# Scores on VectorE, no unread TensorE products after the first step, and a new order on every engine

## The chip, the cores and the metric

The kernel runs on one core of a Trainium2 chip. The metric is the time of the whole program on the device, in microseconds (us), as the median of several runs. Lower is better.

## What is computed

The reference is two adaptive-norm layers over 16 batch elements of 256 tokens and 128 channels, all in float32. Each layer has an attention part and a feed-forward part, and both are added back with a gate:

```python
h = _layernorm(x) * (1 + ca) + sa
x = x + ga * _L0_attn_ref(h, ...)      # 16 heads of 8 channels, softmax over 256 keys
h = _layernorm(x) * (1 + cb) + sb
x = x + gb * _L0_ffn_ref(h, ...)       # 16 experts, top 4 of them weighted by a softmax
...
h = _layernorm(x) * (1 + ca) + sa
x = x + ga * _L1_attn_ref(h, ...)      # running sums over time of value * phase rotor
h = _layernorm(x) * (1 + cb) + sb
x = x + gb * _L1_ffn_ref(h, ...)       # token shift, sigmoid and squared relu
```

The change touches the expert part of the first layer. All 16 experts are computed for every token, and the top-4 scores (zero for the other experts) scale each expert's hidden activation:

```python
gate = jnp.minimum(gu[..., ::2], LIMIT)
up = jnp.clip(gu[..., 1::2], -LIMIT, LIMIT)
glu = gate * jax.nn.sigmoid(gate * ALPHA)
act = (up + 1.0) * glu
expert_out = jnp.einsum('tei,eih->teh', act, down_proj) + down_bias
out = jnp.einsum('te,teh->th', scores, expert_out)
```

## The kernel before

Everything lies in on-chip memory as 128 channels by 256 tokens, one batch element at a time. The program is a software pipeline of three batch elements. A step(a, b, nx) runs the attention and the experts of element a (layer 0), the whole second layer of element b = a - 1, and the start of element nx = a + 1: its load, first norm, the q and k products, and the first scores. There is a head and a `first` for element 0, then `step(1, 0, 2)`, a hardware loop `Fori(2, 15)` with 13 passes, `step(15, 14, None)`, and `last(15)`.

Nothing schedules the work at run time. Each engine runs the calls of its own `step` in the order in which they are written, and an instruction waits at the head of its engine's queue until the semaphores that `need(...)` names have come. So the order of the calls is the schedule. The pieces that matter here:

- **Attention of a.** `scores(n)` and `maxima(n)`, n = 0 to 7: TensorE makes four heads of scores at a time in one half of the PSUM tile `ring`, VectorE (DVE in the profile) reduces them to row maxima `smax`. `split_max`, `turn_max`, `copy_max` and the DMA `spread_max` put the maxima into two rows of `q_rows`. Then `scores_t(n)`, `exps(n)` (ScalarE, ACT in the profile) and `values(n)`. `copy_values` writes `o_raw`, which is a part of `sc_all`. `turn_values`, `attn_norm`, `attn_out_1/2`, `attn_tail/attn_tail_2` and GpSimd's `residual1` end it in `x1`.
- **Rows of nx.** For the scores q and k have to stand three times over in bf16 parts on other partitions. ACT's `part` and `part_2` and GpSimd's `rest_q` and `rest_q_2` make the parts `qk_part`, and `spread(nx)` on the SyncE queue (SPq) issues 18 DMAs of 64 KB into `q_rows` and `k_rows`. `scores(nx, 0)` waits for all 18.
- **Router and experts of a.** Second norm, `router`, `route`/`route_2` on VectorE make the scores `sc` and their three bf16 parts; `turn_scores` and `copy_scores` turn them; `broadcast(n)` spreads the scores of four experts over the partitions and `copy_broadcast(n)` copies them to `sc_all`. For each pair n of experts: TensorE's `gate_up(n)` into `ring`, ACT's `gate_clip`, `bend` (silu, into `gsc`), `up` and `clip_up` (into `upc`, a part of `prob`), GpSimd's `expert_pair(n)` multiplies `gsc` by `sc_all`, VectorE's `expert_last(n)` multiplies by `upc`, and TensorE's `down_pair(n)` sums into `pa`. `experts_out` ends it in `x2`, and the third norm (`mean`, `centre3`, `square`, `variance`, `epsilon`, `deviation`, `scale`, `modulate`) gives the second layer its input `hb`.
- **Second layer of b.** Four column groups c = 0 to 3: `phases`/`phase`/`memory_a`/`tables` make the sines and cosines, `phase_values`/`value` and `time_values` the values, `memory_p/_b/_c/_d/_o/_s/_s12` on VectorE and `sums_1/2` on TensorE the running sums, `memory_wo(c)` adds the projection into `pb`. `memory_end`, the fourth norm and `mix_...` end it.
- **Unread products.** `warm(n, bank)` runs n float32 products of 256 columns whose result nobody reads. A step has five of them: two in `warm_scores` and three (`WARM`) in `broadcast(a, 0, nx)`. `warm_last` adds ten in the step without nx.

A float32 product of 256 columns shows as two passes on TensorE (PE). GpSimd (POOL) cannot read PSUM, and reads `gsc` and `sc_all` from SBUF, as VectorE can. The two calls that swap engines and the fillers in question are these:

```python
def expert_pair(b, n):                     # POOL, line 421
    need(pool, "silu", b, n + 1)
    if n % 2 == 0:
        need(pool, "bc", b, n // 2 + 1)
...
def warm_scores(b, n):                     # PE, line 722
    need(pe, "ya", b, 1)
    warm(n, ring[:, 1, :])
```

## Time and profile before

| what | value |
|---|---|
| runs | 1394.96, 1395.64 and 1398.1 us |
| median | 1395.64 us |
| span of the profiled execution | 1390.0 us |
| the profiled execution's own time | not listed apart from the three runs; the median is 5.6 us over the span |
| PE busy | 1248.1 us, 90% of the span |
| VectorE busy | 1136.3 us, 82% |
| ACT busy | 970.5 us, 70% |
| POOL busy | 280.8 us, 20% |
| mean granted TensorE clock | 0.994 of full speed |
| one pass of the loop | 81.2 us |

How to read it. The span runs from the first to the last instruction; what the median has beyond it is launch and end. PE's share is high, but its busy time holds the unread products as well. A busy share alone does not tell what ends a step: the engines wait for each other in a fixed order, so the places where PE stands still, and what ends each of these waits, tell more than the shares.

### The profile page before, as it was taken

What the parts mean: (1) busy time and instruction counts of PE and PEld (TensorE: products, weight loads), DVE (VectorE), ACT (ScalarE), POOL (GpSimd) and SP (SyncE); (2) the same over time, 40 slices, a digit from 0 to 9 for tenths busy, and PEclk for the clock granted to TensorE, in tenths of its full rate; (3) what the DMA queues carried; (4) which work ended last, traced back from release to release, by engine and by line L of the source; (5) the groups of instructions that cost most, each with busy time, mean ns of one, the idle gap of its engine ahead of it and who ended that gap; (6) DMA issues with size and microseconds to landing.
All of it is one profiled execution on the core that took longest, in us unless ns stands there. A gap on an engine that the chain in (4) does not pass through costs nothing.

```text
span 1390.0 us, 22686 instructions
## 1 busy us (share of the span) xinstructions
PE 1248.1 (90%) x7130; PEld 938.9 (68%) x7130; DVE 1136.3 (82%) x2104; ACT 970.5 (70%) x1699; POOL 280.8 (20%) x258
## 2 busy tenths in 40 slices
PE   7798998989899898989989898998989899898989
PEld 5475775758577575757758575775857577585778
DVE  7758879797987979798797979879797987979765
ACT  1665767778676777867677786767778676776841
POOL 4030221303022130302213031221303122130200
PEclk9899999999999999999999999999999999999999
DMA  5330301204030110403012030301204030120000
GB/s 126 93 35 5 35 9 16 20 8 34 8 34 8 15 19 8 34 8 32 10 13 21 8 34 8 31 10 13 21 8 34 8 31 11 12 22 5 1 4 4
DMA packets 54392, 29.82 MB, mean 21 GB/s; under 512 B 3725, under 2 KB 53338, under 8 KB 54362
## 3 DMA queue, kind: packets, MB, share of 16 engines
q1 hardware_dynamic: 52472, 28.74, 17.2%
q10 hardware_dynamic: 1890, 0.70, 0.5%
q8 instruction: 16, 0.26, 0.1%
q14 instruction: 14, 0.11, 0.0%
HBM read 8.20 MB, written 2.10 MB: 7 GB/s over the span
## 4 chain that ended last, share of the span: by engine, by line
PE 56%; DVE 14%; ACT 14%; issue 10%; POOL 2%; DMA 1%; SPq 1%; ACTq 1%; DVEq 0%; POOLq 0%
PE ring L762 15%; PE pb L862 7%; PE pa L776 7%; DVE smax L1814 5%; PE pa L680 4%; PE ring L667 3%; PE ring L716 3%; PE pb_k L792 2%; DVE prod L1927 2%; ACT prob L1279 2%; PE ring L749 2%; PE ring L629 2%; PE pb_v L820 1%; ACT L1383 1%; ACT frac L1386 1%
## 5 line engine op out<-in xcount | busy, mean ns | idle before, releaser
L427 POOL TENSOR_TENSOR gsc<-gsc,sc_all 128x512 f32<-128x512 f32 x128 | 175.7, 1377 | 353.2 <-ACT gsc L1344 353.2
L762 PE MATMUL ring<-ht,wgu 128*128 128x256 f32 x1024 | 241.5, 384 | 1.0 <-ACT sc_all L1332 1.0
L1954 DVE TENSOR_TENSOR_SCAN prod<-keep,prod 128x512 f32<-128x512 f32 x188 | 224.2, 1214 | 0.0
L762 PEld LDWEIGHTS ring<-ht,wgu 128*128 128x128 f32 x1024 | 193.2, 191 | 34.8 <-issue 5.0
L1814 DVE TENSOR_REDUCE smax<-ring 128x4 f32<-128x1024 f32 x128 | 153.3, 1219 | 17.6 <-PE ring L629 10.8
L1887 DVE SCALAR_TENSOR_TENSOR prob<-prob,gsc 128x512 f32<-128x512 f32 x120 | 81.4, 688 | 81.9 <-POOL gsc L427 63.5
L862 PE MATMUL pb<-prod,wo 128*128 128x256 f32 x544 | 129.3, 382 | 5.9 <-DVE prod L1968 5.8
L1279 ACT ACTIVATE prob<-ring 128x1024 f32<-128x1024 f32 x128 | 125.7, 1024 | 5.1 <-PE ring L667 3.5
L1339 ACT ACTIVATE gsc<-ring,gub_t 128x256 f32<-128x256 f32 x256 | 110.5, 501 | 21.3 <-PE ring L762 21.0
L776 PE MATMUL pa<-prob,wdown 128*128 128x256 f32 x512 | 122.0, 380 | 1.8 <-DVE prob L1881 1.8
L862 PEld LDWEIGHTS pb<-prod,wo 128*128 128x128 f32 x544 | 102.0, 190 | 25.2 <-DVE prod L1968 12.0
L1350 ACT ACTIVATE prob<-ring,gub_t 128x256 f32<-128x256 f32 x240 | 103.5, 499 | 8.9 <-PE pa L776 7.0
L776 PEld LDWEIGHTS pa<-prob,wdown 128*128 128x128 f32 x512 | 95.9, 190 | 15.3 <-DVE prob L1881 3.0
L1344 ACT ACTIVATE gsc<-gsc,gate_top 128x512 f32<-128x512 f32 x128 | 95.1, 760 | 0.3
L1355 ACT ACTIVATE prob<-prob,up_top 128x512 f32<-128x512 f32 x120 | 87.5, 770 | 0.0
L680 PE MATMUL pa<-prob,vt 128*32 128x256 f32 x1024 | 76.9, 394 | 10.3 <-ACT prob L1279 8.4
L667 PE MATMUL ring<-q_rows,k_rows 128*128 128x256 bf16 x512 | 73.7, 277 | 11.8 <-ACT prob L1279 10.4
L1332 ACT ACTIVATE sc_all<-ring 128x1024 f32<-128x1024 f32 x64 | 63.5, 1023 | 23.4 <-DVE prod L1949 16.2
L792 PE MATMUL pb_k<-hb,wk 128*128 128x256 f32 x256 | 68.6, 390 | 12.2 <-ACT hb L1242 11.5
L667 PEld LDWEIGHTS ring<-q_rows,k_rows 128*128 128x128 bf16 x512 | 42.8, 98 | 49.9 <-ACT prob L1279 29.6
L629 PE MATMUL ring<-k_rows,q_rows 126*128 126x256 bf16 x480 | 70.2, 276 | 6.3 <-ACT prob L1350 3.0
L420 POOL TENSOR_TENSOR x<-xt,ya 128x256 f32<-128x256 f32 x16 | 11.6, 727 | 305.0 <-ACT ya L1306 305.0
(284 smaller groups left out, 2476.1 us busy)
## 6 DMA issues: line engine op xcount, KB each, us to landing
q_rows<-qk_part SPq DMA_DIRECT2D x144, 64.0 KB
k_rows<-qk_part SPq DMA_DIRECT2D x135, 64.0 KB
x_in<-in_L_attn_x_dram SPq DMA_DIRECT2D x16, 128.0 KB, 2.1
sc_all<-_L_ffn_gate_up_proj_dram SPq DMA_DIRECT2D x1, 2048.0 KB, 11.9
out_dram<-xo SPq DMA_DIRECT2D x16, 128.0 KB, 1.8
prob<-in_L_wmod_dram SPq DMA_DIRECT2D x2, 384.0 KB, 3.9
k_rows<-qk_part ACTq DMA_DIRECT2D x9, 64.0 KB
wo<-in_L_attn_Wo_dram SPq DMA_DIRECT2D x1, 512.0 KB, 7.4
```

What stands on the lines that cost most here:

```text
L427: pool.tensor_tensor(gsc[:, n % NG, :], gsc[:, n % NG, :], sca, ALU.mult).then_inc(S["gsc"], 1)
L629: last = mm(ring[:, n % 2, j * L:(j + 1) * L], lhsT=q_rows[0:P - 2, h, (n // 4) * P:(n // 4 + 1) * P], rhs=k_rows[0:P - 2, h, :], start=Tr ...
L667: last = mm(ring[:, (n + 1) % 2, j * L:(j + 1) * L], lhsT=k_rows[:, h, (n % 2) * P:(n % 2 + 1) * P], rhs=q_rows[:, h, :], start=True, stop ...
L680: last = mm(pa[32 * j:32 * (j + 1), o:o + L], lhsT=vt[:, n % 2, 4 * (n // 2) + j, :], rhs=prob[:, n % NPT, j, :], start=(n % 2 == 0), stop ...
L762: last = mm(ring[:, n % 2, g * 512 + j * L:g * 512 + (j + 1) * L], lhsT=wgu[:, 2 * n + j, g, :], rhs=ht[:, :], start=True, stop=True, skip ...
L776: last = mm(pa[:, 0:L], lhsT=wdown[:, 2 * n + j, :], rhs=upc[:, n % NU, j * L:(j + 1) * L], start=False, stop=(n == 7 and j == 1), skip_gr ...
L862: last = mm(pb[:, 0:L], lhsT=wo[:, n // 2, 2 * c + j, :], rhs=prod[:, c % 2, n, j * L:(j + 1) * L], start=(c == 0 and n == 0 and j == 0), ...
L1279: af(prob[:, n % NPT, :, :].rearrange("p i q -> p (i q)"), ring[:, (n + 1) % 2, :], ACT.Exp).then_inc(S["prob"], 1)
L1339: af(gsc[:, n % NG, j * L:(j + 1) * L], ring[:, n % 2, j * L:(j + 1) * L], ACT.Relu, scale=-1.0, bias=gub_t[:, 0, 2 * n + j:2 * n + j + 1] ...
L1350: af(upc[:, n % NU, j * L:(j + 1) * L], ring[:, n % 2, 512 + j * L:512 + (j + 1) * L], ACT.Relu, scale=-1.0, bias=gub_t[:, 1, 2 * n + j:2 ...
L1814: nc.vector.tensor_reduce(smax[:, n // 4, 4 * (n % 4):4 * (n % 4) + 4], ring[:, n % 2, :].rearrange("p (h k) -> p h k", h=4), AX_X, ALU.ma ...
L1954: nc.vector.tensor_tensor_scan(prod[:, h, n - 1, :], keep[:, :], prod[:, h, n - 1, :], 0.0, ALU.mult, ALU.add).then_inc(S["cu" + str(n)], 1)
```

## The change

Four things are changed.

1. In every step the product of silu and spread score, `gsc * sc_all`, is made by VectorE (`expert_mul`) in place of GpSimd (`expert_pair`). `first` keeps GpSimd's.
2. `warm_scores` and `broadcast` run their unread products only for element 0, so each of the 15 steps has five fewer. `warm_last` is gone (ten in the last step). In `last` four are moved to its start, four between the mean and the variance are dropped, and four stand behind the last transposes in place of ahead of them.
3. The calls of every engine are put in another order.
4. The boundary of the loop pass lies elsewhere: `scores(nx, 7)`, `turn_max(nx)` and the first `phases`, `phase_values` and `time_values` of the second layer end a step, where they began the next one. VectorE's `scale(.., "3", ..)`, `next_b` and `maxima(.., 4)` begin a step, where they ended one.

The waits that were calls of their own (`rows_landed`, `values_free`, `weights_loaded`, `tables_ready`, `weights_copied`) stand inside the calls that need them, for element 0.

```diff
@@ gpsimd, step
                 if on_x:
                     rest_q(nx)
                     rest_q_2(nx)
-                if on_a:
-                    expert_pair(a, 0)
...
-                    expert_pair(a, 6)
                 if on_b:
                     deviation(b, "4", vepsb, rstdb)
                 if on_a:
-                    expert_pair(a, 7)
                     deviation(a, "3", vepsb, rstdb)
@@ vector
+            def expert_mul(b, n):
+                need(dve, "silu", b, n + 1)
+                need(dve, "bc", b, n // 2 + 1)
+                sca = sc_all[:, 2 * n:2 * n + 2, :].rearrange("p e t -> p (e t)")
+                tt(gsc[:, n % NG, :], gsc[:, n % NG, :], sca, ALU.mult).then_inc(S["gsc"], 1)
@@ tensor
             def warm_scores(b, n):
                 need(pe, "ya", b, 1)
-                warm(n, ring[:, 1, :])
+                if is_first(b):
+                    warm(n, ring[:, 1, :])
...
-                    warm(WARM, ring[:, 0, :])
+                    if is_first(b):
+                        warm(WARM, ring[:, 0, :])
@@ tensor, first
-                turn_max(a)
                 turn_inv()
                 turn_bias()
+                turn_max(a)
@@ sync, step
-                if nx is not None:
+                if on_a:
+                    spread_max(a)
+                if on_x:
                     load_x(nx)
-                if a is not None:
-                    spread_max(a)
-                if nx is not None:
                     spread(nx)
```

The rest of the diff is the order of the calls. Three places of it are shown as the instructions of the loop pass.

The first is ACT's queue from the router to the experts, before the change. `qk_part<-qk` is `part` and `part_2`, `sin_t`, `frac`, `cos_t` are `tables(b, 3)`, `sctb` and `sct` are `copy_scores`, and `sc_all<-ring` is `copy_broadcast`.

```order
L1259 ACTIVATE qk_part<-qk 128x512
L1242 ACTIVATE ht<-cent,mod_a 128x256
L1264 ACTIVATE qk_part<-qk 128x512
L1375 ACTIVATE sc_all<-pb_k 128x512
L277 REGISTER_ALU
L1317 ACT_TABLE_LOAD
L1317 ACTIVATE ex<-lsh 128x32
```

And the same place of ACT's queue after it, from `route` on:

```order
L1298 ACTIVATE ex<-lsh 128x32
L1299 ACT_TABLE_LOAD
L1299 ACTIVATE silu<-gate_top 128x1
L1364 ACTIVATE sin_t<-frac 128x2x256
L1367 ACTIVATE frac<-frac 128x512
L1371 ACTIVATE cos_t<-frac,half_pi 128x2x256
L287 REGISTER_ALU
L1241 ACTIVATE qk_part<-qk 128x512
L287 REGISTER_ALU
L1304 ACTIVATE sctb<-ring 48x256
L1306 ACTIVATE sct<-ring 16x256
```

`part` stood ahead of `route`'s exponential and stands behind it and behind `tables(b, 3)` now. `part_2` moves further, to between the third and the fourth copy of the spread scores:

```order
L1313 ACTIVATE sc_all<-ring 128x1024
L1246 ACTIVATE qk_part<-qk 128x512
L287 REGISTER_ALU
L1313 ACTIVATE sc_all<-ring 128x1024
L287 REGISTER_ALU
L1320 ACTIVATE gsc<-ring,gub_t 128x256 x2
```

So the rows of nx can only be issued once three of the four score copies are through, just ahead of the first `gate_clip`.

The second place is PE's queue between the router and the first `gate_up`. Before (`ring<-upper,ident` are the unread products, `pb<-prod,wo` is `memory_wo`, `ring<-sctb,sel` is `broadcast`):

```order
L716 MATMUL ring<-upper,ident 128x256 x2
L862 MATMUL pb<-prod,wo 128x256 x4
L731 MATMUL ring<-ident,sc 16x128 x2
L733 MATMUL ring<-identb,sc_part 48x128 x2
L716 MATMUL ring<-upper,ident 128x256 x3
L749 MATMUL ring<-sctb,sel 128x256 x8
L827 MATMUL pb_k<-upper,prod 128x256
```

And after it:

```order
L859 MATMUL pb<-prod,wo 128x256 x4
L824 MATMUL pb_k<-upper,prod 128x256
L826 MATMUL pb_k<-upper,prod 128x128
L824 MATMUL pb_k<-upper,prod 128x256
L826 MATMUL pb_k<-upper,prod 128x128
L727 MATMUL ring<-ident,sc 16x128 x2
L729 MATMUL ring<-identb,sc_part 48x128 x2
L746 MATMUL ring<-sctb,sel 128x256 x4
```

The running sums `sums_1(b, 2)` (`pb_k<-upper,prod`) moved ahead of the turned scores, and no product stands where the five unread ones were.

The third place is VectorE's queue in the expert stage, after the change (`gsc<-gsc,sc_all` is `expert_mul`, `prob<-prob,gsc` is `expert_last`, `prod<-keep,prod` is a scan of `memory_c`):

```order
L1870 TENSOR_TENSOR gsc<-gsc,sc_all 128x512
L1942 SCALAR_TENSOR_TENSOR prod<-keep,prod 128x512 x2
L1875 SCALAR_TENSOR_TENSOR prob<-prob,gsc 128x512
L287 REGISTER_ALU
L1870 TENSOR_TENSOR gsc<-gsc,sc_all 128x512
L1927 TENSOR_TENSOR prod<-prod,cos_r 128x512
L1875 SCALAR_TENSOR_TENSOR prob<-prob,gsc 128x512
L1942 SCALAR_TENSOR_TENSOR prod<-keep,prod 128x512
```

Each `expert_last` now has its own `expert_mul` ahead of it on the same queue, most with one or two pieces of the second layer between them.

## Rows read from the trace of the kernel before

**Rows 1.** Page, the span and part 1, busy us of each engine.

```profile
span 1390.0 us, 22686 instructions
...
PE 1248.1 (90%) x7130; PEld 938.9 (68%) x7130; DVE 1136.3 (82%) x2104; ACT 970.5 (70%) x1699; POOL 280.8 (20%) x258
```

**Rows 2.** Windows: sum, PE, PEld, DVE, ACT, POOL, clock, DMA share, GB/s; one pass.

```profile
600.40:681.60 81.20, 73.74 (x430) 55.15 (x429) 68.62 (x126) 60.34 (x107) 16.80 (x15) 1.00 0.17 18
```

**Rows 3.** Timeline, start and us, around the two groups of unread products.

```profile
639.56 1.03 PE L716 MATMUL ring<-upper,ident 128*128 128x256 f32 x4
...
641.01 1.99 PE L862 MATMUL pb<-prod,wo 128*128 128x256 f32 x8 [0.41 <-DVE prod L1968]
...
643.60 1.56 PE L716 MATMUL ring<-upper,ident 128*128 128x256 f32 x6
...
644.43 0.36 ACT L1323 ACTIVATE sctb<-ring 48x256 bf16<-48x256 bf16 x1
...
645.10 1.04 PE L749 MATMUL ring<-sctb,sel 48*128 48x256 bf16 x8
```

**Rows 4.** Groups by line and shape: busy, mean ns, idle before.

```profile
L1887 DVE SCALAR_TENSOR_TENSOR prob<-prob,gsc 128x512 f32<-128x512 f32 x120 | 81.4, 688 | 81.9 <-POOL gsc L427 63.5 <-ACT prob L1355 18.2
...
L1974 DVE TENSOR_TENSOR prod<-prod 128x512 f32<-128x512 f32 x60 | 41.0, 684 | 0.0
```

**Rows 5.** Timeline, a POOL product beside a VectorE product, both from SBUF.

```profile
659.10 1.64 POOL L427 TENSOR_TENSOR gsc<-gsc,sc_all 128x512 f32<-128x512 f32 x1 [0.88 <-ACT gsc L1344]
659.53 1.77 DVE L1962 TENSOR_TENSOR prod<-prod,cos_t 128x512 f32<-128x512 f32 x1
```

**Rows 6.** Timeline, nine places of one pass.

```profile
609.50 0.71 SPq L308 DMA_DIRECT2D q_rows<-m_sb  x1
...
612.00 1.04 PE L667 MATMUL ring<-q_rows,k_rows 128*128 128x256 bf16 x8
...
614.59 4.98 ACT L1279 ACTIVATE prob<-ring 128x1024 f32<-128x1024 f32 x5
...
624.67 0.60 ACT L1295 ACTIVATE sc_all<-pa 128x512 f32<-128x512 f32 x1 [0.76 <-PE pa L680]
...
630.49 0.72 POOL L420 TENSOR_TENSOR x<-xt,ya 128x256 f32<-128x256 f32 x1 [19.69 <-ACT ya L1306]
...
638.36 0.19 DVE L1836 TENSOR_TENSOR lg<-ring,rbias 128x32 f32<-128x32 f32 x1 [0.21 <-PE ring L707]
...
649.30 3.72 PE L762 MATMUL ring<-ht,wgu 128*128 128x256 f32 x16
...
672.98 1.03 PE L629 MATMUL ring<-k_rows,q_rows 126*128 126x256 bf16 x8 [0.21 <-ACT prob L1350]
...
678.66 0.41 DVE L1759 TENSOR_TENSOR centb<-x,pb 128x256 f32<-128x256 f32 x1
```

**Rows 7.** Timeline, the last part of q and k and the first DMA of rows.

```profile
638.25 1.16 POOL L414 TENSOR_TENSOR qk_part<-qk,qk_part 128x512 bf16<-128x512 f32 x1 [1.29 <-ACT qk_part L1264]
...
639.43 0.63 SPq L303 DMA_DIRECT2D q_rows<-qk_part  x1
```

**Rows 8.** Windows, end of the row DMAs issued from 476.93 and 720.69 on.

```profile
496.93:497.93 1.00, 1.00 (x7) 0.87 (x6) 1.00 (x2) 1.00 (x4) 1.00 (x1) 1.00 0.18 13
...
744.69:745.69 1.00, 1.00 (x6) 0.90 (x5) 0.00 (x0) 1.00 (x4) 1.00 (x1) 1.00 0.08 4
```

**Rows 9.** First step: timeline, then a window behind that wait, clock 0.61.

```profile
38.53 0.29 PE L546 MATMUL pb<-ident,gsc 16*128 16x16 f32 x2 [1.02 <-DVE gsc L1696]
...
107.30 1.78 PE L629 MATMUL ring<-k_rows,q_rows 126*128 126x256 bf16 x8 [1.26 <-DMA k_rows<-qk_part]
...
107.30:108.00 0.70, 0.70 (x4) 0.52 (x5) 0.00 (x0) 0.00 (x0) 0.00 (x0) 0.61 0.00 0
```

**Rows 10.** Timeline, the last step: a rstd and the products that wait behind fillers.

```profile
1328.31 0.69 POOL L402 TENSOR_TENSOR rstdb<-vepsb,mhalf 128x2 f32<-128x2 f32 x1 [5.25 <-DVE vepsb L1763]
...
1329.71 0.61 PE L584 MATMUL pb<-ident,rstdb 128*128 128x128 f32 x4
```

More of the change, by code:

```diff
@@ L959, in step @@
                 if on_b:
-                    memory_wo(b, 0)
+                    phases(b, 3)
                 if on_x:
-                    head_3(nx)
+                    head_1(nx)
                 if on_a:
@@ L1133, in first @@
                 scores(nx, 5)
+                phases(a, 0)
+                phase_values(a, 0)
                 scores(nx, 6)
-            def last(b):
-                phases(b, 0)
-                phase_values(b, 0)
-                phases(b, 1)
-                time_values(b, 0)
-                phase_values(b, 1)
+                scores(nx, 7)
+                time_values(a, 0)
+                phases(a, 1)
+                turn_max(nx)
+                phase_values(a, 1)
+            def last(b):
+                warm(4, ring[:, 0, :])
                 time_values(b, 1)
@@ L1477, in step @@
                     tables(b, 3)
+                if on_x:
+                    part(nx)
                 if on_a:
@@ L1557, in first @@
                 copy_broadcast(a, 2)
+                part_2(nx)
                 copy_broadcast(a, 3)
-                part(nx)
-                part_2(nx)
                 gate_clip(a, 0)
@@ L2026, in step @@
                 on_a, on_b, on_x = a is not None, b is not None, nx is not None
+                if on_b:
+                    scale(b, "3", centb, pb)
+                    next_b(b)
                 if on_a:
+                    maxima(a, 4)
                     maxima(a, 5)
-                    maxima(a, 6)
+                    next_a(a)
                 if on_b:
@@ L2156, in step @@
                     maxima(nx, 3)
-                    maxima(nx, 4)
                 if on_b:
                     mix_out(b)
-                if on_a:
-                    scale(a, "3", centb, pb)
-                    next_b(a)
             def first(a, nx):
@@ L2215, in first @@
                 maxima(nx, 3)
-                maxima(nx, 4)
-                scale(a, "3", centb, pb)
-                next_b(a)
             def last(b):
+                scale(b, "3", centb, pb)
+                next_b(b)
                 memory_a(b, 0)
```

419 lines of the change are left out of this document (204 added, 215 removed).

## The prediction, on record before the run

> **What bounds the kernel now.** I read the busy times first. PE is busy for 1248 of 1390 us, VectorE for 1136, POOL for 281 [rows 1]. One pass of the hardware loop takes 81.2 us and holds 73.7 us of PE, 68.6 of VectorE, 60.3 of ACT and 16.8 of POOL, at full TensorE clock [rows 2]; so PE stands still for 7.5 us of a pass and VectorE for 12.6. No engine is full, and the end of a pass is set by a chain that changes engine. I therefore read the idle time by line, then the timeline of one pass. I measure places in it from the third norm's first instruction (`centre3`, 678.66 here, so 597.41 one period of 81.25 earlier) [rows 6]. On that scale the softmax exponentials start at 17.2, the second `copy_values` is at 27.3, POOL's residual `x` at 33.1, the router's logits at 40.9, the first `gate_up` at 51.9, the first scores of nx at 75.6, the next `centre3` at 81.25.
>
> **The expert products.** One of VectorE's waits stands out: 63.5 us of the 81.9 ahead of `expert_last` end with POOL's product, which is 63.5 / 15 = 4.2 us a step [rows 4]. VectorE now gets eight products of its own. A product of 128x512 f32 from SBUF took it 0.684 us [rows 4], so 8 x 0.684 = 5.5 us are added. POOL loses its eight. Where both read SBUF at once, a VectorE product took 1.77 us in place of 0.68 and POOL's 1.64 [rows 5]; this one collision a pass gives back 1.1. VectorE goes from 68.6 to about 73.0 us a pass. What hides it is the 12.6 us that VectorE idles [rows 2], 4.2 of them just these waits for POOL. That cover is thin in the expert stage; were it gone, the net cost would be 5.5 - 1.1 - 4.2 = 0.2 us a pass. I take zero, since PE has 22 us of products queued there.
>
> The Trainium skill (SBUF — State Buffer, two separate sides) calls the shared port pair an exclusive lock: the loser waits for the whole instruction. By it up to eight of POOL's products could each block VectorE for one, and the relief would be up to eight times 1.1, 8.8 us. The trace shows one stretched VectorE product in a pass, so it does not bear that out.
>
> **The unread products.** Five f32 products are ten PE passes, 1.03 + 1.56 = 2.6 us a step [rows 3]. But PE's next product behind the first group waits 0.41 us for VectorE even with them, and the turned scores behind the second group are ready at 644.43 + 0.36 = 644.79, against the product's 645.10 [rows 3]. So at most 0.3 us of the second group is on the path. PE goes to 73.7 - 2.6 = 71.1 us a pass. The gain is bounded by zero and 2.6; I take 0.3, and it is inside the walk below.
>
> **The new order, up to the experts.** I walked each engine's new queue with the durations of the old timeline.
> - Exponentials: 17.2 to 16.0. VectorE's `scale` and `next_b` stand ahead of the fifth maxima, so `hb` comes 1.2 us earlier and ACT's sines no longer end last. What is late next is the DMA of maxima rows, 2.5 us from its issue to PE's use [rows 6].
> - From there to the second `copy_values`: 10.05 to 9.9. ACT's phases leave the gap between exponentials, but PE's running sums stand behind the second turned scores and cost 0.35.
> - To POOL's `x`: 5.85 to 5.1, because the sine table load no longer stands ahead of the attention output.
> - To the logits: 7.85 to 7.3. VectorE's copy of x is out of the norm; a `memory_wo` on PE ahead of the norm's last product costs about 0.8 of that again.
> - To the first `gate_up`: 10.95 to 11.2. Here ACT has `tables(b, 3)` (2.0 us) and `part` (0.6) ahead of `copy_scores`, which eats what the unread products gave.
>
> Together the first `gate_up` starts 2.4 us earlier, at 49.5. Behind it PE had 23.7 us until the scores of nx (672.98 - 649.30 [rows 6]) and has 22.05 now, with the bias products moved ahead and one variance moved out. So PE could start these scores at 71.55, in place of 75.6.
>
> **The rows of nx: the new wait.** Before, the last part of q and k ended at 639.41, on my scale 42.0, and the first of 18 row DMAs was issued at once [rows 7]. Issue to landing took between 20.75 and 24.2 us in 13 passes, 22.6 in the mean; the shortest and the longest end in [rows 8]. They landed some 11 us before PE used them, so nothing waited. Now `part` stands behind the router's exponential and `tables(b, 3)`, and `part_2` behind three of four score copies. By my walk the last part ends at 51.15, 1.65 us after the first `gate_up`. The rows land at 51.15 + 22.6 = 73.75, and `scores(nx, 0)`, ready at 71.55, waits 2.2 us. Queued behind it on PE are the down products and the norm of `x2`. On this branch the time from the scores to the next `centre3` is 5.65 + 1.3 = 6.95 us: VectorE's mixing now stands between `experts_out` and `centre3`, and one more group of scores ahead of the mean. The period comes to 73.75 + 6.95 = 80.7 us, against 81.25. That is 0.55 a pass, and for 14 steps with rows 7.7 us. Slips of PE, VectorE or ACT in the expert stage up to 2.2 us cost nothing there, since the rows are awaited anyway.
>
> **Outside the steady passes.** Step 15 has no nx and so no rows: it keeps the whole 2.35 us, and 1.2 for `warm_last` (the reciprocal root is ready at 1329.0, the product behind the fillers runs at 1329.71 [rows 10], and a second group costs as much), 3.5 in all. In `last`, unread products ahead of the variance and of the last transposes go: 1.0. In the first step the rows are issued some 2.7 us earlier, and the wait of 1.26 us at 107.30 goes [rows 9]; `turn_bias` ahead of `turn_max`, near PE's wait at 38.53 [rows 9], delays the maxima, of which 1.2 stays: 1.5 net. Sum 6.0; bounds 2 and 9.
>
> **The clock.** All steady passes ran at full clock, with no PE gap over 1.0 us. In the first step, behind gaps of 0.70, 1.12 and 1.26 us, the granted clock fell: 0.61 of full in the window behind the last one [rows 9], and stayed at 1.2 GHz until 110.8, at a cost of at most 1.7 us. The new row wait of 2.2 us is longer than those gaps, and the unread products that kept PE busy are gone. Bounds: zero, and 1.7 x 14 = 24 us. I take 0.3 a pass, nearer zero because the work on either side of the wait is dense (73.7 of 81.2), which the first step's is not: 4.2 us.
>
> **Sum.** The profiled execution's own time is not listed apart; its span is 1390.0, and the median of the runs, 1395.64, is 5.6 above it. Changes of the span are carried to the median as they stand: 1395.64 - 7.7 - 6.0 + 4.2 = 1386.1, said as 1386.0. The mean row time alone moves it by (24.2 - 22.6) x 14 = 22 us up or (22.6 - 20.75) x 14 = 26 down (down to where PE binds), though single passes average out.
>
> **Rivals.**
> A. *The rows do not bind.* They land as PE wants them, because `part_2` runs earlier than my walk puts it or 18 DMAs go faster beside a quieter POOL. Then the period is 81.25 - 2.35 = 78.9, and the time 1395.64 - 14 x 2.35 - 6 = 1356.7. For it: 11 us of slack before. Against it: the queue's order says plainly that the parts come some 9 us later. Chance 0.13.
>
> B. *The row wait halves the clock: slower.* Place: `scores(nx, 0)`. Each pass then runs what follows at 1.2 GHz, as the first step did from 107.4 to 110.8. At the full 1.7 us a pass, with the late rows eating the 7.7 (they land at 24.2 rather than 22.6, or the parts slip by 0.55 more), the time is 1395.64 + 24 - 6 - 7.7 to + 24 - 6, so 1406 to 1414. It decides as soon as the loss exceeds 1.0 us a pass. For it: [rows 9]. Against it: that was a stage with three gaps near each other. The Trainium skill (TensorE: Matmul & The Clock Gate, section HAM oscillation) tells of a kernel whose TensorE waits for a DMA in every tile and restarts at the low clock each time; by it this is what each pass would do. The first step's rows agree with it, and no row of a steady pass shows a wait that long. Chance 0.22.
>
> C. *VectorE becomes the bound, so the change does not do what it says.* With 73.0 of 80.7 us busy and each `expert_last` behind its product and one or two scans, its queue would set the pace of the down products. Net 0.2 us a pass beyond before, and nothing of the order's gain: 1395.64 + 3 = 1399, less or more by what the ends give. For it: the 63.5 us wait is replaced by work on the same engine. Against it: VectorE has only 0.68 where POOL had 1.64 [rows 5] and a hand-over. Chance 0.10.
>
> My forecast, rows bind and part of the gain stays, has 0.55.
>
> **Numbers.** The range is 1362 to 1408: it leaves out most of A's low end and B's high end. About 0.2%, 2.8 us, is what a measurement of this kernel can tell from no change, so faster means below 1392.8 and slower above 1398.4. Faster gets A's 0.13 and 0.41 of the forecast's 0.55, together 0.54. Same gets 0.10 of the forecast and 0.06 of B and C. Slower gets the rest of B and C, 0.26, and 0.04 of the forecast: 0.30.
>
> **What would show it.** Right: a period near 80.7; a wait of about 2 us for a DMA at PE's first scores of nx, in every pass but the last; the first `gate_up` 49.5 after `centre3`, the last part 1.6 behind it; the third norm starting 7 us behind these scores; PE near 71, VectorE near 73 and POOL near 6 us a pass; no wait of `expert_last` for POOL; the product that took 1.77 back at 0.68; granted clock near 1.00. Wrong: no DMA wait there (A), a clock clearly under 1.00 in steady passes (B), PE waiting for `prob` from VectorE through the expert stage (C), or `gate_up` not earlier than 51.

## The result, and the profile after

The changed kernel takes 1419.8 us (median of four runs, 1410.5 to 1439.2), the kernel before 1395.6. The ratio, 1.0146 with a 95% interval of 1.0125 to 1.0168, is of the fast runs alone and leaves out the one of 1439.2. So the change is slower by 20 us by the ratio and by 24 by the medians. The forecast was 1386, range 1362 to 1408, with 0.30 for slower.

The page, span and busy times:

```profile
span 1420.3 us, 22302 instructions
...
PE 1268.9 (89%) x6960; PEld 951.5 (67%) x6960; DVE 1212.2 (85%) x2224; ACT 971.2 (68%) x1699; POOL 137.9 (10%) x138
```

Against [rows 1], VectorE grew by 76 us and POOL halved, both in the direction foreseen. VectorE takes 73.9 us a pass, not 73.0: the 1.1 us of relief did not come. The product that took 1.77 us is back at 0.68, but in the pass from 613.14 two others now run beside GpSimd's `rest_q` and `rest_q_2` and take 1.65 and 1.13 us in place of 0.68. And PE is 21 us busier with 170 products fewer. The windows of two passes, measured from `centre3` to `centre3` (columns as in [rows 2]: clock, DMA share and GB/s at the end), say why:

```profile
526.63:613.14 86.51, 76.24 (x419) 57.04 (x419) 73.89 (x135) 60.38 (x107) 7.20 (x7) 0.92 0.18 17
...
866.94:947.87 80.93, 74.01 (x419) 55.09 (x419) 73.81 (x135) 60.39 (x107) 7.21 (x7) 0.96 0.16 18
```

The granted clock is 0.92 to 0.96 in every steady pass, where it was 1.00 [rows 2], and passes of one program now take anything from 80.9 to 86.7 us. The 14 passes with rows take 1163.6 us together, 83.1 each, against 81.2. That is 27 of the 30 us between the spans; the first step adds 1.3 us and step 15 another 2.0. The spans lie further apart than the medians because the profiled execution of the kernel before was a short one. In every run listed with its span the time is only 1.7 or 1.8 us above the span, so of the 5.6 us between span and median of the kernel before some 4 are that difference and not launch and end. Its granted clock of 0.994 is above the 0.988 to 0.993 of the same kernel's later runs too. PE's longest waits, in all, how often, and the longest:

```profile
PE ring L620 <- DMA k_rows<-qk_part: 18.6, 12, 5.1
PE ring L661 <- DMA q_rows<-m_sb: 18.0, 15, 1.3
PE ring L746 <- ACT sc_all L1313: 15.5, 20, 1.2
PE ring L746 <- ACT sctb L1304: 15.1, 15, 1.1
```

There are three places a pass: the first scores of nx (L620), the first turned scores, waiting for the maxima rows (L661), and the spread scores (L746), where the unread products stood. The timeline at the three, the last two in the pass from 866.94, the first in that from 526.63:

```profile
880.59 1.05 PE L661 MATMUL ring<-q_rows,k_rows 128*128 128x256 bf16 x8 [1.15 <-DMA q_rows<-m_sb]
...
911.24 0.59 PE L746 MATMUL ring<-sctb,sel 48*128 48x256 bf16 x4 [1.07 <-ACT sctb L1304]
...
603.92 1.46 PE L620 MATMUL ring<-k_rows,q_rows 126*128 126x256 bf16 x6 [3.33 <-DMA k_rows<-qk_part]
```

And the windows behind the last two of these:

```profile
913.94:919.94 6.00, 6.00 (x17) 3.78 (x18) 5.93 (x10) 3.27 (x4) 1.16 (x1) 0.50 0.06 14
...
603.86:610.00 6.14, 6.08 (x23) 5.11 (x24) 2.67 (x5) 0.29 (x1) 0.69 (x1) 0.50 0.00 0
```

Both run at 0.50, which is 1.2 GHz. Such a stretch is called a drop below. One stands at the spread scores in every pass and takes in the first `gate_up`; one at the first turned scores comes in nine of 15 passes; one at the row wait in the four that waited over 1.5 us. Neither of the first two places has a single wait: PE stands still for 0.57, 0.66 and 1.15 us within 4 us at the turned scores of the pass from 866.94, and for 1.07 and 0.88 us within 4 us at its spread scores.

The last reading is of the rows. SPq issued the first at 577.46. Windows around their end:

```profile
601.00:602.00 1.00, 0.00 (x0) 0.00 (x0) 0.90 (x2) 0.93 (x3) 0.00 (x0) 1.00 0.41 24
602.00:603.00 1.00, 0.00 (x0) 0.00 (x0) 0.00 (x0) 0.00 (x0) 0.00 (x0) 1.00 0.00 0
603.00:604.00 1.00, 0.08 (x1) 0.09 (x2) 0.00 (x0) 0.00 (x0) 0.00 (x0) 0.64 0.00 0
```

The queues fall silent before 602.0, some 24 us behind the issue, which is the long end of [rows 8]. PE starts at 603.92, about 2 us behind the last packet, and for most of that time no engine works. The trace also keeps the times of the semaphore updates that the transfers send, though no view lists them. Over the 14 passes with rows the last one comes 22.2 to 26.4 us behind the issue, 24.2 in the mean, which is 1.0 to 2.1 us behind the last packet. Where PE waits it starts 0.05 us behind that update. From issue to PE it is 26.5 us here, and 24.6 to 26.5 in the four passes that waited over 1.5 us.

VectorE's groups, as in [rows 4]:

```profile
L1870 DVE TENSOR_TENSOR gsc<-gsc,sc_all 128x512 f32<-128x512 f32 x120 | 82.4, 688 | 49.6 <-ACT gsc L1325 49.4
...
L1875 DVE SCALAR_TENSOR_TENSOR prob<-prob,gsc 128x512 f32<-128x512 f32 x120 | 82.2, 685 | 3.2
```

The 63.5 us of waiting for POOL are gone. VectorE now waits for ACT and is not the bound.

### The profile page after: what moved, and what is told of

It reads as the page before. It is cut to its first block, busy times and chain, and to the rows that moved or that the text cites. A ratio compares the mean times of both kernels' runs of the same rounds, so it can differ in the third digit from the quotient of the medians.

```text
span 1420.3 us, 22302 instructions
## 1 busy us (share of the span) xinstructions
PE 1268.9 (89%) x6960; PEld 951.5 (67%) x6960; DVE 1212.2 (85%) x2224; ACT 971.2 (68%) x1699; POOL 137.9 (10%) x138
## 4 chain that ended last, share of the span: by engine, by line
PE 40%; DVE 16%; DMA 14%; ACT 10%; SPq 9%; issue 8%; POOL 3%; ACTq 0%; DVEq 0%; POOLq 0%
DMA k_rows<-qk_part 11%; SPq L313 9%; PE ring L661 4%; PE ring L759 4%; PE pb L859 4%; PE pa L773 4%; DVE prod L1937 4%; PE pa L676 3%; DVE smax L1796 3%; PE pb_k L789 3%; DMA q_rows<-m_sb 2%; PE pb_v L824 2%; ACT prob L1261 1%; DVE prod L1910 1%; PE ring L620 1%
## 5 line engine op out<-in xcount | busy, mean ns | idle before, releaser
L759 PE MATMUL ring<-ht,wgu 128*128 128x256 f32 x1024 | 266.1, 414 | 1.1
L759 PEld LDWEIGHTS ring<-ht,wgu 128*128 128x128 f32 x1024 | 212.1, 210 | 48.5 <-issue 14.2
L773 PE MATMUL pa<-prob,wdown 128*128 128x256 f32 x512 | 133.4, 396 | 0.0
L1870 DVE TENSOR_TENSOR gsc<-gsc,sc_all 128x512 f32<-128x512 f32 x120 | 82.4, 688 | 49.6 <-ACT gsc L1325 49.4
L1331 ACT ACTIVATE prob<-ring,gub_t 128x256 f32<-128x256 f32 x240 | 110.1, 556 | 0.1
L859 PEld LDWEIGHTS pb<-prod,wo 128*128 128x128 f32 x544 | 101.0, 190 | 12.5
L1325 ACT ACTIVATE gsc<-gsc,gate_top 128x512 f32<-128x512 f32 x128 | 105.3, 824 | 0.2
L661 PE MATMUL ring<-q_rows,k_rows 128*128 128x256 bf16 x512 | 81.6, 298 | 21.4 <-DMA q_rows<-m_sb 18.0
L1336 ACT ACTIVATE prob<-prob,up_top 128x512 f32<-128x512 f32 x120 | 95.3, 816 | 0.0
L661 PEld LDWEIGHTS ring<-q_rows,k_rows 128*128 128x128 bf16 x512 | 47.0, 105 | 63.3 <-issue 42.0
L620 PE MATMUL ring<-k_rows,q_rows 126*128 126x256 bf16 x480 | 67.6, 280 | 18.7 <-DMA k_rows<-qk_part 18.6
L1224 ACT ACTIVATE hb<-centb,mod_b 128x256 f32<-128x256 f32 x32 | 19.2, 601 | 94.4 <-DVE centb L1749 57.9
L412 POOL TENSOR_TENSOR rstdb<-vepsb,mhalf 128x2 f32<-128x2 f32 x32 | 22.5, 703 | 562.5 <-DVE vepsb L1745 562.5
```

The lines of the kernel that those rows point to most:

```text
L661: last = mm(ring[:, (n + 1) % 2, j * L:(j + 1) * L], lhsT=k_rows[:, h, (n % 2) * P:(n % 2 + 1) * P], rhs=q_rows[:, h, :], start=True, stop ...
L759: last = mm(ring[:, n % 2, g * 512 + j * L:g * 512 + (j + 1) * L], lhsT=wgu[:, 2 * n + j, g, :], rhs=ht[:, :], start=True, stop=True, skip ...
L773: last = mm(pa[:, 0:L], lhsT=wdown[:, 2 * n + j, :], rhs=upc[:, n % NU, j * L:(j + 1) * L], start=False, stop=(n == 7 and j == 1), skip_gr ...
L859: last = mm(pb[:, 0:L], lhsT=wo[:, n // 2, 2 * c + j, :], rhs=prod[:, c % 2, n, j * L:(j + 1) * L], start=(c == 0 and n == 0 and j == 0), ...
L1325: af(gsc[:, n % NG, :], gsc[:, n % NG, :], ACT.Silu, scale=-ALPHA, bias=gate_top[:, 0:1]).then_inc(S["silu"], 1)
L1331: af(upc[:, n % NU, j * L:(j + 1) * L], ring[:, n % 2, 512 + j * L:512 + (j + 1) * L], ACT.Relu, scale=-1.0, bias=gub_t[:, 1, 2 * n + j:2 ...
```

## The experiments

All kernels are stated against the kernel before, run on the same chip beside them (1395.9 to 1397.2 us).

**First four: the unread products and the late rows, one by one.** `after_fillers_back` puts the five products of a step back.

```diff
 def warm_scores(b, n):
     need(pe, "ya", b, 1)
-    if is_first(b):
-        warm(n, ring[:, 1, :])
+    warm(n, ring[:, 1, :])
@@ broadcast, n == 0
-                    if is_first(b):
-                        warm(WARM, ring[:, 0, :])
+                    warm(WARM, ring[:, 0, :])
@@ tensor, step
                     sums_2(b, 2)
+                if on_a:
+                    warm_scores(a, 2)
+                if on_b:
                     memory_wo(b, 1)
```

> The changed kernel with the five unread products of every step put back where they stood (two ahead of the turned scores, three ahead of the first spread of scores). Theory A (the clock: the wait of 1.07 us ahead of the spread scores, where the unread products stood, drops TensorE to 1.2 GHz for 6.8 us in every pass, and this is the larger cost): the drop behind the turned scores is gone in every pass, PE's busy time falls by 2 to 3 us a pass although work is added, and the time is 1385 to 1400 us. Rival B (the row wait is the main cost, the clock hardly matters): the clock comes back, but the time stays at 1410 us or more, since the rows are issued at the same place. Rival C (VectorE is the bound): no change, 1415 to 1425.

Its four runs took 1412.6, 1441.8, 1448.0 and 1459.1 us. Rival B's bound, 1410 us or more, held: in the profile, which is of the shortest run, the clock is back at 0.94 to 0.98 a pass, and the time is no better. PE is earlier at the scores of nx and the rows are not, so it waits longer there (22.8 us in all, against 18.6), and four passes have a drop at that wait, which is on the path. Whether this kernel is slower than the changed one is open, since its shortest run lies among the changed kernel's.

`after_parts_early` issues the rows earlier, at 48.2, where passes of the changed kernel with a drop at the turned scores issue them at 52.5 and those without at 50.8.

```diff
                 if on_a:
                     route(a)
-                if on_b:
-                    tables(b, 3)
                 if on_x:
                     part(nx)
+                if on_b:
+                    tables(b, 3)
                 if on_a:
                     copy_scores(a)
-                    copy_broadcast(a, 0)
-                    copy_broadcast(a, 1)
-                    copy_broadcast(a, 2)
                 if on_x:
                     part_2(nx)
                 if on_a:
+                    copy_broadcast(a, 0)
+                    copy_broadcast(a, 1)
+                    copy_broadcast(a, 2)
                     copy_broadcast(a, 3)
```

> The changed kernel with part directly behind the router's exponential, ahead of the last tables, and part_2 directly behind copy_scores, ahead of all four copies of the spread scores; no unread products. The rows are issued some 5 us earlier. Theory A (clock at the score turn is the larger cost): the DMA waits of 18.6 us at the first scores of nx go to under 2, with the clock drops behind them, but the drop behind the turned scores stays in every pass: 1398 to 1410 us. Rival B (rows are the main cost): 1385 to 1395 us. Rival C (VectorE): 1415 or more.

1403.9 us (1400.9 to 1406.2), ratio 1.0045 [1.0028, 1.0062], as theory A had it. The row waits of the passes are gone (4.7 us stay in the first step) and so is the spread of the runs. But nearly every pass took 81.9 us at a clock of 0.94, with a drop at the turned scores and one at the spread scores in every one.

> Both edits. Theory A: no row wait, and no clock drop but one behind the wait for the maxima rows: the period comes near 79.5 us and the time to 1370 to 1380 us. Rival B: the same as with the early parts alone, within 3 us. Rival C (VectorE is the bound at 73.5 us busy): not under 1395.

This has both edits. 1408.3 us, ratio 1.0081 [1.0064, 1.0097]: neither theory A's 1370 to 1380 nor within rival B's 3 us. Rival C's bound, not under 1395, is met, and the next pair of runs tells against it. One pass, and the clock behind the wait for the maxima rows and around the last spread of scores:

```profile
602.66:684.55 81.89, 76.25 (x429) 57.13 (x429) 74.20 (x134) 60.54 (x107) 7.19 (x7) 0.96 0.17 18
615.50:619.00 3.50, 2.69 (x11) 2.05 (x12) 3.50 (x6) 3.47 (x5) 0.00 (x0) 0.57 0.15 39
651.50:655.30 3.80, 3.23 (x13) 1.96 (x13) 3.77 (x8) 2.85 (x3) 0.00 (x0) 0.77 0.47 64
```

Two drops were left, behind a wait of 1.14 us for the maxima rows and behind one of 0.57 us ahead of the last spread. That made the next pair of edits.

`before_no_fillers` is the kernel before with `if` b is element 0 ahead of both `warm` calls, as the change has it.

> The kernel before with nothing changed but the five unread products of a step left out (those of the first step stay, and the ten of the last step). Theory A (the unread products hold the clock): a wait of 1 us or more appears on PE ahead of the spread scores, the clock falls behind it in most passes, and the time is 10 to 35 us over the kernel before, 1405 to 1430. Rival (they only matter in the new order, whose queue of ACT is later there): clock stays full, 1391 to 1397 us, as the 0.3 us a step of the prediction says.

1404.6 us (1400.6 to 1411.1), ratio 1.0061 [1.0031, 1.009], just under the low edge of theory A. Its timeline and two of its passes:

```profile
480.51 1.96 PE L864 MATMUL pb<-prod,wo 128*128 128x256 f32 x8 [1.38 <-DVE prod L1970]
...
484.35 1.03 PE L751 MATMUL ring<-sctb,sel 48*128 48x256 bf16 x8 [1.27 <-ACT sctb L1325]
```

```profile
436.79:522.74 85.95, 76.30 (x420) 56.70 (x419) 68.78 (x126) 60.61 (x107) 16.13 (x15) 0.94 0.18 17
...
605.44:686.54 81.10, 71.46 (x420) 53.55 (x419) 69.62 (x126) 60.39 (x107) 16.29 (x15) 1.00 0.18 18
```

The waits of 1.38 and 1.27 us stand in every pass of the loop, where the unread products had covered all but 0.41 us of them. In seven of the 13 loop passes the clock holds and the pass is 81.1 us, 0.15 shorter than before, which is what the prediction's 0.3 was about. In five it falls, and they take 82.7 us, in one more 86.0. The products are worth having for the clock alone.

**Second four: fill the two places, then move the expert products.** `maxima_filled` adds two products.

```diff
                 if n == 0:
...
-                    need(pe, "m_rows", b, 16)
                     need(pe, "s_max", b, ST)
+                    warm(2, ring[:, 1, :])
+                    need(pe, "m_rows", b, 16)
```

> after_fillers_and_parts with two more unread products on PE in every step, behind the last maxima and ahead of the wait for the maxima rows (1.2 us in which PE stands still, behind which the clock fell in every pass there). Theory A (the clock drops, not the waits, hold this order back): the drop 12 to 13 us after centre3 is gone, the exponentials start about 1.7 us earlier after it, and with the second drop staying the period is 80.2 us, the time 1380 to 1388 us. Rival B (the pass is bound by VectorE, 74 us busy, or by its waits; the clock is only a symptom): the period stays 81.9 us and the time within 3 us of 1408.

1371.6 us (1367.7 to 1379.5), ratio 0.9838 [0.9793, 0.9884]: 37 us for two products that nobody reads, more than theory A gave. The wait of 1.14 us is 0.25 now, no pass has the drop behind it, and seven of the 13 loop passes have no drop at all, though the wait of 0.57 us ahead of the last spread is still in each. Theory A had the second drop stay everywhere. The timeline at that wait, a pass without a drop and one with the second:

```profile
599.75 1.03 PE L712 MATMUL ring<-upper,ident 128*128 128x256 f32 x4
601.02 1.05 PE L662 MATMUL ring<-q_rows,k_rows 128*128 128x256 bf16 x8 [0.25 <-DMA q_rows<-m_sb]
```

```profile
587.40:666.10 78.70, 73.95 (x433) 55.84 (x433) 73.96 (x135) 60.46 (x107) 7.19 (x7) 1.00 0.17 19
666.10:746.01 79.91, 75.25 (x433) 57.16 (x433) 74.10 (x134) 60.77 (x107) 7.19 (x7) 0.98 0.17 18
```

`maxima_and_spread_filled` moves a real product into the other wait.

```diff
                     broadcast(a, 2)
-                    broadcast(a, 3)
                     down_bias(a)
+                    broadcast(a, 3)
```

> maxima_filled with down_bias moved ahead of the last spread of scores, where PE waited 0.57 us for ACT's copy. Theory A: both drops are gone in every pass, granted clock 1.00, period 78.5 to 79.5 us, time 1357 to 1372 us. Theory A2 (the products of 48 rows there leave TensorE too little work, whatever the wait): the second drop stays, as in maxima_filled within 3 us. Rival B: the period stays 81.9 us.

1358.5 us (1356.3 to 1361.3), ratio 0.9732 [0.9704, 0.976]. Theory A, in all its numbers for the loop (step 15 keeps a drop of 6.8 us):

```profile
582.68:661.19 78.51, 73.93 (x433) 55.85 (x433) 73.97 (x135) 60.55 (x107) 7.19 (x7) 1.00 0.18 19
```

All 13 passes of the loop run at full clock and take 78.4 to 78.5 us, with VectorE busy for 74.0 of them. So VectorE was not the bound at 81.9, which rules out rival B here and rival C of the first four. The second drop did not stay, where theory A2 had expected it to. The moved product fills the wait and puts other work between the products of 48 rows at once, so this pair of runs does not part the two.

`filled_pool_products` gives the eight products of a step back to GpSimd, where the kernel before has them.

```diff
@@ gpsimd, step
                     rest_q_2(nx)
+                if on_a:
+                    expert_pair(a, 0)
...
+                    expert_pair(a, 7)
@@ vector, step
-                if on_a:
-                    expert_mul(a, 0)
...
-                    expert_mul(a, 7)
```

> maxima_and_spread_filled with the eight products of silu and spread score back on GpSimd in the steps (expert_pair), nothing else. If the move to VectorE is what helps (it removed 4.2 us a step of waits for POOL): 10 to 30 us slower than maxima_and_spread_filled. If VectorE at 74 us busy had become the bound: faster by 5 us or more. If the expert stage is bound by PE either way: within 3 us.

1413.4 us, ratio 1.0122 [1.0092, 1.0151]: 55 us slower, beyond the first case's 30. Its group on VectorE:

```profile
L1886 DVE SCALAR_TENSOR_TENSOR prob<-prob,gsc 128x512 f32<-128x512 f32 x120 | 122.4, 1030 | 58.6 <-POOL gsc L437 58.6
```

VectorE waits 58.6 us for POOL again, and its own product takes 1030 ns in the mean instead of 688 [rows 4]. The two engines now meet in the expert stage more often than once a pass: in the pass from 607.93 five VectorE products of 0.68 us take 1.70 to 1.77. That is what the Trainium skill (SBUF — State Buffer, two separate sides) says of the shared port pair, and the row agrees in kind: 342 ns more for each of 120. Passes at full clock take 81.8 us, 3.3 more than 78.5; that is 46 of the 55 us. Four of the 13 loop passes have a drop besides, so not all of the 55 is the expert stage.

`before_products_dve` makes only that part of the change: each product directly ahead of its `expert_last`, in the old order. The other seven pairs are moved as the one shown.

```diff
@@ vector, step
+                    expert_mul(a, 0)
                     expert_last(a, 0)
...
@@ gpsimd, step
-                    expert_pair(a, 0)
...
```

> The kernel before with only the eight products of silu and spread score moved to VectorE, each directly ahead of its expert_last; old order, all unread products. The prediction's 0.2 us a pass at most (5.5 added, 4.2 and 1.1 had back): 1391 to 1399 us. Rival (each product stands on VectorE's path because the second layer's pieces behind it come later): 1405 us or more.

1424.1 us, ratio 1.0184 [1.0149, 1.022]: 27 us slower, the rival. A pass and the group that waits:

```profile
615.15:698.08 82.93, 74.51 (x430) 55.12 (x429) 72.53 (x134) 60.52 (x107) 5.81 (x7) 1.00 0.18 18
```

```profile
L1884 DVE SCALAR_TENSOR_TENSOR prob<-prob,gsc 128x512 f32<-128x512 f32 x120 | 83.1, 692 | 45.4 <-ACT prob L1346 35.9 <-DVE gsc L1879 3.1
```

The clock is full in every pass of the loop. A pass is 1.7 us longer, and all of it lies behind the first `gate_up`, which starts at 51.9 as before: the scores of nx start at 76.6 instead of 75.6, and the next `centre3` another 0.7 later. Over 14 passes that is 24 us. `expert_last` still waits 45.4 us, now for ACT. So the products on VectorE cost 27 us in the old order, and giving them back costs 55 in the new one, which was written for them.

**Last six: the prices, taken from the good side.** `filled_no_five` takes the five products out again, `filled_parts_late` puts `part` and `part_2` back where the change has them; both edits were shown above the other way round.

> maxima_and_spread_filled without the five unread products at the score turn; the two at the maxima wait, the early parts and down_bias ahead of the last spread stay. What the five are worth in this order. The prediction's price (0.3 us a step had back by leaving them out): 2 to 6 us faster than maxima_and_spread_filled. The clock theory: the wait of 1.1 us ahead of the spread scores comes back, the clock falls behind it for 3.4 to 6.8 us in every pass, and the time is 1380 to 1400 us, at least 20 us slower.

1389.6 us (1387.5 to 1390.0), ratio 0.9947 [0.993, 0.9963], 31 us slower. The wait ahead of the spread scores is back, and with it the clock:

```profile
803.75 0.59 PE L747 MATMUL ring<-sctb,sel 48*128 48x256 bf16 x4 [1.07 <-ACT sctb L1305]
```

```profile
759.45:840.69 81.24, 74.55 (x423) 55.93 (x423) 74.26 (x135) 60.38 (x107) 7.62 (x7) 0.96 0.17 18
```

> maxima_and_spread_filled with part and part_2 back where the change has them (behind the last tables, and between the third and fourth copy of the spread scores). What the late rows cost where no other place drops the clock. The prediction's step (the rows are issued 51 us after centre3, land 22.6 us later and bind): a DMA wait of 2 us or more at the first scores of nx in most passes, a period of 80.5 us or more, and the clock falling behind the longer waits: 1385 to 1405 us. Rival (the rows do not bind, rival A of the prediction): within 5 us of maxima_and_spread_filled.

1431.9 us (1412.2 to 1451.0), ratio 1.0169 [1.0104, 1.0235]; all four runs are above the 1405 expected. PE waits for the rows in all 14 passes that have them, and in the first step; the profile is of its longest run:

```profile
PE ring L620 <- DMA k_rows<-qk_part: 59.7, 15, 6.3
```

To part the wait from the clock behind it, two kernels add unread products to `filled_parts_late`, ahead of the wait for the rows:

```diff
-                if n == 0:
-                    need(pe, "qk_rows", b, 16 * 18)
...
+                if n == 0:
+                    warm(6, ring[:, 0, :])
+                    need(pe, "qk_rows", b, 16 * 18)
```

> filled_parts_late with six more unread products on PE ahead of the wait for the rows (2.6 us, about the shortest of the waits there). It parts the wait from the clock that falls behind it. If the wait itself is the price of the late rows (issue at 51.05, PE let go 24.6 to 26.5 us later, against 71.9 where PE could start, and 6.6 us from there to the next centre3, 82.3 to 84.2 us a pass): 1410 to 1432 us, the clock in the passes at 0.98 or more, and only 0 to 20 us had back. If the clock behind the wait is the larger part of it: 1395 us or less.

> The same with ten products (4.3 us). PE is then free at 76.2 us, near the middle of the landings: clock 1.00 in nearly every pass, a remaining wait under 1 us on average. If the wait is the price: within 8 us of the run with six, 1405 to 1430 us. If the clock is: further down with the second drop gone, 1395 us or less.

1404.7 us with six (ratio 1.0064 [1.0046, 1.0082]), 1421.3 with ten (1.0189 [1.0169, 1.021]). The late rows cost 73 us by the medians and 61 by the ratios; six products bring 27 or 15 of that back, which lies between my two cases. The products themselves can only hold PE up, and only one drop at the row wait is left, so part of the price was the clock. How large a part is not shown: between the two profiles the rows also got faster, from 25.3 us to 24.3 in the mean from issue to last semaphore update, some 13 us over 14 passes. What remains is the 2.6 us of products in each pass (36 us), 6.7 us of waits, and a drop at the spread scores in eight passes. Ten are longer than most of the waits and cost 17 us again: inside the first case's range, though not within 8 us of the run with six.

`after_maxima_filled_only` is the changed kernel with the two products of maxima_filled and nothing else.

> The changed kernel with nothing but two unread products ahead of the wait for the maxima rows. The drop 12 to 13 us after centre3, which came in about half of the passes, is gone; the one at the score turn and the row wait stay. Theory (each drop costs about half its length, but where the rows bind, time had back earlier only lengthens the row wait, since gate_up and part_2 hang on the same score copies): 1405 to 1420, no clear difference from the changed kernel. Rival (it is the maxima wait that started the trouble): under 1400.

1399.5 us (1384.2 to 1408.6), ratio 1.001 [0.998, 1.0041]. The theory's 1405 was too high and the rival's bound is just met: two unread products alone bring the changed kernel back to the time of the kernel before, 19 us by the ratios and 20 by the medians. The drop at the score turn in every pass and row waits of 0.6 to 3.1 us in eight are still in its profile, which is of its longest run.

The last tries for more, at both ends of the program.

```diff
@@ act, first
                 route(a)
+                part(nx)
                 down_scaled()
                 copy_scores(a)
-                part(nx)
+                part_2(nx)
                 copy_broadcast(a, 0)
                 copy_broadcast(a, 1)
                 copy_broadcast(a, 2)
-                part_2(nx)
@@ tensor, step
+                if on_a and not on_x:
+                    need(pe, "norm2", a, 1)
+                    warm(2, pa[:, L:2 * L])
                 if on_a:
                     broadcast(a, 1)
```

> maxima_and_spread_filled, with part and part_2 of the first step moved ahead in the same way as in the steps, and two unread products in the last step where head_6 has no work. The row wait of 8.5 us in the first step falls to about 5, and the clock drop in the middle of the last step is gone: 3 to 7 us faster than maxima_and_spread_filled, 1352 to 1356 us. If the rows of the first step land no earlier, or the drop only moves: within 2 us.

1356.8 us (1352.8 to 1358.1), ratio 0.9712 [0.9691, 0.9733]. The first step ends 5.9 us earlier. But two passes had a row wait of 1.1 us that the profile of maxima_and_spread_filled does not have, and two others a drop, so most of it did not stay. The drop in the middle of the last step is gone, and a shorter one stands at its end. By its number this is the second case, within 2 us, and the intervals of the two overlap. Both are 2.7 to 2.9% faster than the kernel before, and some 4% faster than the change.

The drop in the loop is worth a look, since both waits are filled there. PE's longest wait ahead of it, and the windows before it and in it:

```profile
1100.02 0.67 PE L767 MATMUL pa<-sct,dbias 16*128 16x256 f32 x2 [0.37 <-DVE vt L1796]
```

```profile
1097.60:1101.10 3.50, 3.13 (x21) 1.75 (x19) 3.50 (x5) 2.96 (x3) 0.81 (x1) 1.00 0.18 38
1101.10:1104.50 3.40, 3.40 (x10) 2.72 (x9) 3.33 (x6) 1.02 (x1) 0.00 (x0) 0.50 0.66 47
```

What PE ran before it fell were mostly the spread's products of 48 rows and `down_bias` with 16. The same calls with the same wait kept the clock in the other 12 passes of the loop. So a wait of 1 us is not needed for a drop, and theory A2 has a part in this place that no run here parts from the waits.

## Why the prediction was wrong

**The walk was right to within 1.3 us a stage, and in part by luck.** Where the first drop is absent the exponentials start at 15.2, the second `copy_values` at 25.2, the residual at 30.3, the logits at 37.5 and the first `gate_up` at 50.0, and at 49.4 once the waits are filled; foreseen were 16.0, 25.9, 31.0, 38.3 and 49.5. The last part of q and k ends at 50.8 against 51.15. In maxima_and_spread_filled the scores of nx start at 71.9, against 71.55 for PE without a wait, and the next `centre3` comes 6.6 us behind them, against 6.95. The stages that were off made up for each other: the exponentials came 0.8 us early, and from the logits to the first `gate_up` it took 12.5 us (11.8 in the filled kernel) for 11.2. Without waits and drops the order is worth in each pass what rival A gave it, a period of 78.5 where it said 78.9. That its 1356.7 us for the whole comes so near the 1358.5 is luck: between the two profiles the passes gave 5.5 us more than it said, and the ends, for which it took off 6.0, cost 2.9. In the changed kernel itself this gain was never had.

**The rows: a term mis-sized.** "The rows land at 51.15 + 22.6 = 73.75." The 22.6 us reached to the last packet. PE is let go by the last semaphore update, 24.2 us behind the issue in the mean. In the kernel before nothing waited for the rows in a steady pass, so no view of those passes showed the 1.7 us between the two; its trace has them (24.3 us in the mean to the last update, against 22.6). With 24.2 the same sum gives 51.15 + 24.2 + 6.95 = 82.3 us a pass, which is 1.05 x 14 = 15 us slower than before, not 7.7 faster. The sign of the likeliest case hung on this term. Of the 83.1 us that a pass took, 51.7 go to the issue, 24.4 from there to PE's start and 7.0 from there to `centre3`. So 1.8 of the 2.4 us by which 80.7 fell short is this term, and 0.6 is the issue, which a drop at the turned scores puts off by 1.7 us in eight of the passes.

**The clock: wrong place and wrong size.** I allowed 0.3 us a pass, behind the row wait alone. The clock fell at waits of 1.07 and 1.15 us too, each with one or two shorter ones within 4 us ahead of it or behind it, in a pass where PE is otherwise busy. The kernel before had one of 1.00 us without a drop, and its nearest wait over 0.5 us is 12 us away. The prediction had put the first step's drop down to "three gaps near each other"; the new order makes such a place at the turned scores of every pass, and I did not look for one. That the nearness decides is not shown: no run moved a neighbour alone. "At most 0.3 us of the second group is on the path" was true of the path and false as a price: the five products are worth 31 us in the filled kernel and 8 in the old order. I had seen that the new order issues nothing where they stood, and that ACT's `tables` and `part` come ahead of `copy_scores`; both make a wait there, and I did not ask what it does to the clock. Rival B named the mechanism and 1406 to 1414 us, but put it only behind the row wait, with 0.22. The Trainium skill (TensorE: Matmul & The Clock Gate, section HAM oscillation) has a case like this, a TensorE that waits for a DMA in every tile and restarts at the low clock. Where the rows bind the changed kernel agrees: the clock fell in all four passes that waited 1.8 us or more for them. But the waits that the page draws there are of 3 to 5 us. It does not say that waits of about 1.1 us drop the clock, and here most of the drops stand at those. My ground for giving it little, that the work on both sides is dense, did not hold.

**The expert products: zero was right for neither order.** The price "5.5 - 1.1 - 4.2 = 0.2" came from busy times and waits of one stage, and its 1.1 was not had back. The runs gave plus 1.7 us a pass in the old order and minus 3.3 in the new one. Rival C did not come true for the change: with 73.9 us of VectorE busy, a pass of 78.5 was possible.

**The ends.** In the first step the rows were issued at 81.74, as foreseen, but PE waited 5.1 us for them and not zero; the step got 1.3 us longer instead of 1.5 shorter. Step 15 took 81.03 us against 79.06, with the clock at 0.94, where I had given it a gain of 3.5.

## What to carry over

Before taking unread work off TensorE, whose clock fell here at waits of about 1 us, look at what waits come to stand in its place, and give each of them a price in clock, also those that are "hidden". Take a DMA's duration to the instruction that it releases, not to its last packet; if nothing waits for it in the profile, add what lies between the two where something does. And a part of a change has no price of its own: test it in the order that it will live in, with the other faults mended.

## What was not expected of the hardware

- The length of a wait alone does not say whether the clock falls. The same 1.15 to 1.26 us ahead of the turned scores stood in all 15 passes of the changed kernel and dropped it in nine; in the two kernels with a period of 81.9 us it did so in 29 of 30. Behind the wait of 0.57 us ahead of the last spread it fell in every pass of after_fillers_and_parts, and in maxima_filled in six of the 13 loop passes. Waits of 1.38 and 1.27 us, 4 us apart, did so in six of the 13 loop passes of before_no_fillers. In the profiled execution of the kernel before a wait of 1.00 us never did, but that was a short execution. At a granted clock of 0.989 the later runs of that kernel spent some 14 us more at half clock (an estimate: 0.005 x 1394 x 2), and no profile shows where. And in filled_ends it fell once in the loop with no wait over 0.37 us near. Which condition decides these runs leave open.
- The spread of a kernel's runs is a sign of its own. The kernels whose PE waits for the rows in most passes spread over 24 to 47 us from run to run; `after_parts_early` and maxima_and_spread_filled over 5. The time from the issue of the rows to their last semaphore update varied as well, from 22.2 to 26.4 us within one execution of the changed kernel.
- In the changed kernel, in passes with rows, 1.0 to 2.1 us pass between the last packet of the 18 row transfers and their last semaphore update, and only 0.05 us between that and the product that waits. What the first part is spent on no run parted.
- VectorE and GpSimd stretch each other outside the expert stage too: in the changed kernel GpSimd's `rstdh` takes 1.53 us beside a scan of VectorE in 14 of 16 steps, in place of 0.69.
